# Helical attention on one core: heads taken four apart, feature products first in the scores, clamp and roots moved back

## What is computed

```
q, k, v = x @ Wq.T + bq, x @ Wk.T + bk, x @ Wv.T + bv          # 16 heads of 8 channels
q_hel = einsum('bshd,hed->bshe', qh, Whel) + bhel               # 64 numbers a head and token
k_hel = einsum('bshd,hed->bshe', kh, Whel) + bhel
qn = l2norm(q_hel.reshape(b, s, h, 32, 2)); kn = ...            # 32 unit vectors of 2
# (the two components are then re-paired along the tokens)
helical = einsum('bhpsc,bhptc->bhst', qn, kn) / 32
dot = einsum('bshd,bthd->bhst', qh, kh) / sqrt(8)
attn = softmax(0.5 * dot + 0.5 * helical)
out = (attn @ vh).reshape(b, s, e) @ Wo.T + bo
```

## Time and profile before

| | us |
|---|---|
| runs | 4297.06, 4308.48, 4308.74; median 4308.48 |
| profiled execution | 4305.09 |
| its span, first to last instruction | 4303.4 |
| granted TensorE clock, mean of the span | 0.864 |
| busy: PE, DVE, ACT, POOL | 3207.1, 2627.0, 1840.7, 1635.4 |
| phase `lm`, first instruction | 2586.21 |
| phase `lo`, first ACT operation to last DVE operation | 3335.12 to 3350.90 |

### The profile page before, as it was taken

How to read it: one execution, slowest core, us unless ns; L and a number is a source line. 1 busy time by engine, 2 the same in 40 slices (tenths; PEclk the granted TensorE clock), 3 DMA queues, 4 the chain that set the end, 5 groups by cost and what they waited for, 6 DMA issues and landing times. The chain is left out here.

```text
span 4303.4 us, 87712 instructions
## 1 busy us (share of the span) xinstructions
PE 3207.1 (75%) x22928; PEld 2524.5 (59%) x22928; DVE 2627.0 (61%) x8135; ACT 1840.7 (43%) x5245; POOL 1635.4 (38%) x2885
## 2 busy tenths in 40 slices
PE   6999999999973849999964756777776685333176
PEld 5888888888862737777753624555554473222155
DVE  5666666666651466666651535666664456999954
ACT  4555556555541325555531324555554333111123
POOL 2222222222216624444427604333432250666533
PEclk9999999999985979999975877888888797666578
DMA  8100000000011310000003200000000120000003
GB/s 138 27 0 4 4 4 1 4 4 0 4 31 57 92 27 2 5 2 4 3 31 89 78 5 17 18 16 18 18 18 14 42 61 20 1 1 1 1 18 90
DMA packets 154383, 104.45 MB, mean 24 GB/s; under 512 B 26160, under 2 KB 144192, under 8 KB 153984
## 3 DMA queue, kind: packets, MB, share of 16 engines
q1 hardware_dynamic: 141056, 75.70, 8.2%
q0 software_dynamic: 13184, 27.19, 1.8%
HBM read 45.86 MB, written 43.87 MB: 21 GB/s over the span
## 5 line engine op out<-in xcount | busy, mean ns | idle before, releaser
L351 POOL TENSOR_TENSOR aa_prob<-aa_prob,aa_inv 128x128 f32<-128x128 f32 (+1 forms) x512 | 249.2, 508 | 919.2 <-DVE aa_inv L567 919.2
L661 POOL TENSOR_TENSOR ab_prob<-ab_prob,ab_inv 128x128 f32<-128x128 f32 (+1 forms) x512 | 248.8, 507 | 334.2 <-DVE ab_inv L816 327.6
L374 PE MATMUL aa_proj<-aa_xs,aa_w 128*128 128x256 f32 x1280 | 362.3, 398 | 13.6 <-DMA aa_w<-in_L_attn_a_W_qkv 12.2
L784 ACT ACTIVATE ab_prob<-ab_ps_score,ab_low 128x128 f32<-128x128 f32 (+1 forms) x512 | 211.7, 424 | 303.6 <-PE ab_ps_turn L718 301.6
L482 ACT ACTIVATE aa_qkv<-aa_proj 128x512 f32<-128x512 f32 x384 | 229.4, 597 | 259.1 <-PE aa_proj L374 198.4
L1778 POOL TENSOR_TENSOR lm_sq<-lm_comp 128x512 f32<-128x512 f32 x128 | 161.2, 1259 | 398.7 <-DVE lm_comp L1945 392.4
L2238 PE MATMUL dr_bank<-da_rT,da_spread 128*128 (+1 forms) x256 | 96.3, 464 | 249.9 <-ACT dr_RW L2256 242.3
L2288 POOL TENSOR_TENSOR dr_toward<-dr_S,XN 128x64 f32<-128x64 f32 x512 | 180.6, 371 | 223.7 <-DVE dr_S L2317 160.8
L1934 DVE TENSOR_REDUCE lm_low<-lm_ps_score 128x2 f32<-128x512 f32 x256 | 164.2, 683 | 152.8 <-PE lm_ps_score L1830 152.8
L374 PEld LDWEIGHTS aa_proj<-aa_xs,aa_w 128*128 128x128 f32 x1280 | 213.8, 191 | 46.0 <-issue 13.8
L540 DVE SCALAR_TENSOR_TENSOR aa_look<-aa_th_look,aa_ahead 128x384 f32<-128x384 f32 x256 | 183.4, 716 | 89.2 <-ACT aa_th_look L488 89.2
(11 more groups left out here) (510 smaller groups left out, 9719.8 us busy)
## 6 DMA issues: line engine op xcount, KB each, us to landing
rt_pairs<-rt_empty SPq DMA_DIRECT2D x2, 4615.0 KB, 44.3
rt_slots<-rt_empty SPq DMA_DIRECT2D x2, 2515.5 KB, 45.0
fa_xin<-rt_back SPq DMA_DIRECT2D x8, 512.0 KB, 7.2
fb_xin<-rt_back SPq DMA_DIRECT2D x8, 512.0 KB, 7.2
lm_staged<-la_stack SPq DMA_DIRECT2D x32, 128.0 KB, 2.2
lm_feat<-la_qk SPq DMA_DIRECT2D x256, 16.0 KB
XN<-lm_outT SPq DMA_DIRECT2D x256, 8.0 KB
XNT<-lm_outT SPq DMA_DIRECT2D x256, 8.0 KB
```

The lines of the kernel that those rows point to most:

```text
L351: ins = nc.gpsimd.tensor_tensor(prob[:, h, a:b], prob[:, h, a:b], inv[:, h, t:t + 1].broadcast_to([P, b - a]), ALU.mult)
L374: ins = nc.tensor.matmul(proj[:, i * SEQ:(i + 1) * SEQ], w[:, m, :], xs[:, k, :], start=True, stop=True)
L661: ins = nc.gpsimd.tensor_tensor(prob[:, h, a:b], prob[:, h, a:b], inv[:, h, t:t + 1].broadcast_to([P, b - a]), ALU.mult)
L784: nc.scalar.activation(prob[:, h, a:b], ps_score[:, h, a:b], ACT.Exp, bias=low[:, h, t:t + 1], accum_out=total[:, h, t:t + 1]).then_inc(ex ...
```

## The change

A turn now takes heads k, k+4, k+8 and k+12 of a batch instead of four neighbours, and the loop is unrolled by four (`KINDS`) instead of two. That lets the whole k side of `feat` be one DMA of 128 rows, and the results stay in `stack` and `qk` (whose columns are used up by then) until SP moves them in groups of four batches; the last group's 48 moves fall in phase `lo`, half on ACT's queue ahead of its first logarithm. `feat` has four buffers, `staged` two, and `wh` is gone. The weights of the layer are loaded at the end of `latent_attention` (class `HelicalWeights`: `load` on SP, `clear` on POOL), so that phase `ls` waits for no DMA.

The diff, cut to what is spoken of:

```diff
@@ latent_attention
                     sp.dma_start(wo[:], w_out[bass.ds(p * P, P), :]).then_inc(wo_in, 16)
+                hw.load(sp, hel_zeroed, hel_loaded)
...
                 nc.gpsimd.tensor_scalar(wqs[:], wqs[:], SCALE, None, ALU.mult).then_inc(wq_scaled, 1)
+                hw.clear(nc, pool, hel_zeroed, hel_picked)
                 pool.wait_ge(lat_ok, CHUNKS)
@@ helical_attention, phase ls
                 def _(pe):
-                    pe.wait_ge(loaded, 128)
...
-                    pe.wait_ge(hloaded, 16 * 4 * HEADS)
                     turn(1)
@@ phase lm, sync
+                    def features(m, b, k):
+                        reached(sp, score_mm, UNITS * (m - 3))
                         for u in range(UNITS):
+                            head = UNITS * u + k
+                            sp.dma_start(feat[32 * u + HD * k:32 * u + HD * k + HD, k, 0, :],
+                                         qk[head * HD:(head + 1) * HD, 0, bass.ds(b * SEQ, SEQ)]).then_inc(feat_ok[k], 16)
+                        sp.dma_start(feat[:, k, 1, :], qk[:, 1, bass.ds(b * SEQ, SEQ)]).then_inc(feat_ok[k], 16)
...
+                    def turn(g, i):
+                        b, k = g * GROUP + i // KINDS, i % KINDS
+                        m = 4 * b + k
+                        if k % 2 == 0:
+                            stage(m, b, k // 2)
+                        features(m, b, k)
+                        if i >= 8 and (not isinstance(g, int) or g > 0):
+                            sp.wait_ge(out_ok, 16 * g)
+                            for n in range(4 * (i - 8), 4 * (i - 8) + 4):
+                                move_out(sp, g - 1, n, moved)
@@ phase lm, tensor
+                    def score(m, k):
+                        j = k % 2
+                        pe.wait_ge(feat_ok[k], 16 * (UNITS + 1) * (m // KINDS + 1))
+                        reached(pe, exp_ok, 8 * m)
+                        for c in range(2):
+                            for u in range(UNITS):
+                                rows = slice(32 * u, 32 * u + 32)
+                                nc.tensor.matmul(ps_score[:, u, c * SEQ:(c + 1) * SEQ], feat[rows, k, 0, c * P:(c + 1) * P],
+                                                 feat[rows, k, 1, :], start=c == 0, stop=False)
                         for i in range(2):
                             pe.wait_ge(unit_ok, 2 * m + i + 1)
-                            reached(pe, exp_ok, 8 * (m - 1) + 4 * i + 4)
...
-                        if live(w, TURNS):
-                            attend(w, 1 - j)
                         if live(a, TURNS):
-                            score(a, 1 - j)
+                            score(a, (k - 3) % KINDS)
+                        if live(w, TURNS):
+                            attend(w, (k - 5) % KINDS)
@@ phase lm, vector
-                        if live(r, TURNS):
-                            clamp(r, 1 - j)
                         if live(a, TURNS):
                             maximum(a, 0)
                             maximum(a, 1)
+                        if live(r, TURNS):
+                            clamp(r, (k - 1) % 2)
@@ phase lo, scalar
                 def _(act):
+                    for i in range(MOVES // 2):
+                        move_out(act, GROUPS - 1, i, moved_too)
                     for c in range(CH):
+                        if c == CH - 2:
+                            act.wait_ge(moved, LANDED // 2)
```

More of the change, by code:

```diff
@@ L1553, in helical_attention @@
+def helical_attention(nc, sh, hw):
     HD, HX = 8, 64
@@ L1580, in helical_attention @@
             CH = TOK // 512
             with nc.Block() as block:
[L1582 to L1610, removed]
@@ L1726, in outputs @@
-                    def outputs(half, b, r):
-                        o = 2 * BATCH * half + 2 * b + r
-                        sp.wait_ge(out_ok, o + 1)
-                        for u in range(UNITS):
-                            head = 8 * half + 4 * r + u
-                            for buf, row in ((heads, 32 * u), (totals, 32 * u + HD)):
-                                sp.dma_start(buf[head * HD:(head + 1) * HD, bass.ds(b * SEQ, SEQ)],
-                                             outT[row:row + HD, r, :]).then_inc(moved[r], 16)
@@ L1736, in stage @@
-                    def stage(n):
-                        reached(sp, hel_mm, 2 * n)
-                        sp.dma_start(staged[:], stack[:, :, bass.ds(n, 1), :].rearrange("p a z s -> p a (z s)")
-                                     ).then_inc(staged_ok, 16)
-                    def step(half, b, last=False):
-                        for r in range(2):
-                            if not isinstance(b, int) or b >= 2:
-                                outputs(half, b - 2, r)
-                            elif half > 0:
-                                outputs(half - 1, b + BATCH - 2, r)
-                            features(half, b, r)
-                            if r == 0 and not last:
-                                stage(half * BATCH + b + 1)
@@ L1752, in _ @@
-                    sp.wait_ge(bare, 1)
-                    stage(0)
-                    for half in range(2):
-                        step(half, 0)
-                        step(half, 1)
-                        with sp.Fori(2, BATCH - 1) as b:
-                            step(half, b)
-                        step(half, BATCH - 1, half == 1)
-                    for b in range(BATCH - 2, BATCH):
-                        for r in range(2):
-                            outputs(1, b, r)
-                    for r in range(2):
-                        sp.wait_ge(moved[r], 16 * 2 * UNITS * (TURNS // 2))
+                            head = UNITS * u + k
@@ L1766, in _, with values @@
+                    sp.wait_ge(bare, 1)
+                    for i in range(16):
+                        turn(0, i)
+                    with sp.Fori(1, GROUPS) as g:
+                        for i in range(16):
+                            turn(g, i)
+                    sp.wait_ge(moved, LANDED * (GROUPS - 1))
                 @block.gpsimd
                 def _(pool):
-                    def values(o, j):
+                    def values(o, k):
                         nc.gpsimd.tensor_copy(
-                            vq[:, j, :, :, 0:HD],
-                            v[:, bass.ds((o // 2) % BATCH * 2, 2), bass.ds((o // (2 * BATCH)) * 64 + 32 * j, 32)]
-                            .rearrange("p t (u d) -> p t u d", d=HD)).then_inc(vq_ok, 1)
+                            vq[:, k % 2, :, :, 0:HD],
+                            v[:, bass.ds(o // 4 * 2, 2), :].rearrange("p t (u k d) -> p t u k d", u=UNITS, k=KINDS)[:, :, :, k, :]
+                        ).then_inc(vq_ok, 1)
@@ L1920, in body @@
                         if live(a, TURNS):
-                            for u in range(UNITS):
-                                exps(a, u)
+                            exps(a, 0)
+                            exps(a, 1)
+                        if live(r, TURNS):
+                            inverse_root(r, (k - 1) % 2)
+                        if live(a, TURNS):
+                            exps(a, 2)
+                            exps(a, 3)
                         if live(o, TURNS):
```

237 lines of the change are left out of this document (140 added, 97 removed).

## The result

The changed kernel takes 4283.29 us (median of 5 runs, 4276.37 to 4287.65), the kernel before in the same comparison 4306.83 (4292.49 to 4308.74): ratio 0.9954, 95% interval 0.9933 to 0.9974. The forecast was 4290, between 4237 and 4348. Timed a second time, beside other kernels, the ratio was 0.9969 (0.9958 to 0.9980). So the change makes the kernel 0.3 to 0.5% faster, as forecast; the terms of the sum came out less evenly than the sum, and a part of the gain lies where none was forecast.

What follows compares the result with a forecast made beforehand. The prediction took the loop's ring of waits through attend, scores, copies and exponentials, plus a price for the clock, to bound the kernel; -14.1 - 6.2 + 1.0 + 3.7 = -15.6 from 4305.1 gave 4290 us, range 4237 to 4348.

Steps and rivals of the forecast that it cites:

- The ring: Loop: the chain of waits through exponentials, roots, features, units, attend, transposes and copy takes 9.61 us against 9.83; -14.1 us.
- The clock's price "as it is": Loop: 1.35 us a turn, for PE's halved clock after idling and for `staged` waits, stays unchanged.
- The moves, `staged` and `wh`, "credited none": Loop: fewer DMAs on SP and more buffers are hidden and gain nothing; bound -20 us.
- The loads: Phase `ls`: without weight loads PE begins at once instead of waiting for the last of eight; -6.2 us.
- The clearing: Before the loop: POOL clears four `feat` buffers instead of two while the first DMAs wait; +1.0 us.
- The clamp: DVE in the loop: put behind two maxima, it still comes in time for the roots; costed at nothing.
- The end: Phase `lo`: ACT issues 24 DMAs before its first logarithm, at 0.65 us each; 28.5 us against 24.8, +3.7 us.
- A: Loop: the price of the clock shrinks and waits for `staged` vanish, around 4250 us; chance 0.25.
- B: Loop: every turn starts at 1.2 GHz, 11.7 to 12.0 us a turn, 4337 to 4356 us; chance 0.25.
- C: Loop: slower exponentials or a late clamp take most of the 14 us gain, 4298 to 4305 us; chance 0.15.

Runs made afterwards that it cites:

- the old orders: The changed kernel with the instruction orders of PE, ACT and DVE put back as in the kernel before: 4289.07 us, 0.9981.
- The late-staged run: The changed kernel with the load of `staged` held back until the helical products of the turn just before are done: 4277.74 us, 0.9940.
- the two kernels with orders alone: The kernel before with only the change's PE, ACT and DVE orders, 4328.23 us, 1.0051; the same with roots behind all exponentials, 4337.29 us, 1.0071.
- filling PE's gap: The changed kernel with each turn's four helical products made twice, as surplus work for PE: 4210.23 us, 0.9783.
- late roots: The changed kernel with the two roots behind all eight exponentials instead of in their middle: 4136.93 us, 0.9625.

## Why the forecast was right, step by step

**The ring** was right: 9.61 forecast, 9.52 to 9.54 found, 9.80 with the old orders in the same surroundings. The shape was right too: taking the 1.28 us of roots out of it gave 1.06 a turn.

**The clock's price "as it is"** is the step that does not hold. With the old orders it is 44.38/4 - 9.80 = 1.30 us a turn, with the new 44.38/4 - 9.54 = 1.56: in the cycle of four turns the price takes up the whole gain of the ring. What the new orders gave the loop, they gave by the pairs of 9.53 and 11.01 that break the cycle in some executions. Timed, they are worth 0.9981 - 0.9954 or 0.9981 - 0.9969, 12 or 5 us, with intervals that overlap; so the -14.1 was too large, and where the orders gained, they gained on the clock's cycle and not by a shorter turn at a fixed price. The kernel before already hinted at that: the 9.83 us of the earlier trace rows, taken for the turn at the high clock, came once in its 63 steps from attend to attend; all others but the last four took 10.9 to 12.5.

**The moves, `staged` and `wh`, "credited none"**, is the term mis-sized the other way. The loop with the old orders is 10 us shorter than before (730.4 for 740.6), half of the bound of 20 that the earlier trace rows gave for the waits for `staged`. That compares one profile with one, while executions of the kernel before ranged over 20 us, from 4291 to 4312; the timed 8 us, with -6.3 for the loads, +10.2 for the end and -7.1 behind the layer, leave some 5 for the loop. The late-staged run shows that the second buffer did not remove the waits; it speaks for SP's shorter queue, which was not isolated. That the orders need the rest of the change shows in the two kernels with orders alone: they lose 22 and 31 us, the second by a late `staged`, the first by a cycle that stays open. The two errors have opposite signs; so the loop's -13.1 was found as -20.8 in one profile and -8.8 in the other.

**Behind the layer** the forecast had no term, and -7.5 to -7.9 us were found. Together with an end that cost 6 us more than forecast, this makes the total a sum of errors that happened to cancel: 4290 was met to 7 us, in part by luck, while the layer alone gave -20.1 in one profile and -5.4 in the other for the forecast's -15.6.

**The loads**: -6.2 forecast, -6 to -9 found. Their hiding place held: SP had issued the last of them at 2175.4, and POOL's last work of that phase ends at 2201.2. **The clearing**: 1.80 for 0.95, +0.9 for the forecast +1.0. **The clamp**: at nothing, as forecast; no wait for it in the changed kernel.

**The end** was mis-sized: +9.8 for +3.7. ACT needed 19.5 us for its 24 DMAs, 0.81 each, not SP's 0.65, and could do nothing else meanwhile. That a second issuing engine saves issuing time and nothing more (the Trainium skill, DMA: Bandwidth & Descriptors, "Issuing engines are not separate DMA queues") fits: 24 on each side took 19.0 and 19.5 us side by side; that it saves nothing more was not tested here. And from the last pair's end, 3325.62, to the last addition's, 3330.27, it took 4.65 instead of 2.62.

**The rivals.** A (a smaller price of the clock) is what other kernels do, by filling PE's gap (70 us) and, for half of its 140 us, by late roots, but not this change. B (every turn slow) came nearest with PE's old order and the roots in the middle, 12.0 to 13.6 us a turn, though one attend in four still ran at full clock there. The rule put behind it (the Trainium skill, TensorE: Matmul & The Clock Gate, "HAM oscillation — how this bites in real kernels") is of a loop whose bursts of products take less time than the waits between them; here PE works 7.18 us of a fast turn of 9.52 and is idle 2.34, so the prediction should not have taken it for this loop, and no run here has its every burst starting at half clock. C is close to what the cycle of four does to the ring's gain.

## What to carry to other kernels

Where an engine's clock follows its idle stretches, the ring of waits at full clock is not yet the time of a turn: ask how long the engine idles in it, and move work that others must wait for out of that gap first; moving 1.3 us of roots was worth 115 to 140 us here. Check a new order together with the queues that feed it: the same order that is 161 us faster than the kernel before with the rest of the change is 31 us slower without it. Profile a kernel with such a clock twice, since a loop of 64 turns came out at 719.7 and 731.8 us with the same code. And compare the profiles outside the changed layer too, over all runs: 7.5 us that could pass for scatter in one pair of profiles were there in every pair.

## What the runs showed of the hardware

In two kernels the granted clock alternated in a fixed cycle of four turns whose sum, 44.38 us, was the same for two rings that differ by 0.26 us a turn. With PE idle 2.34 us ahead of the features the mean clock was 0.86 in one profile and 0.84 in the other of the same code, with 3.4 us (ahead of attend) 0.80, with 1.28 to 1.49 it was 0.98 to 1.00, and 60 us of surplus products were paid back more than once. DMAs issued by ACT took 0.81 us each in a row and SP's beside them 0.79; SP's moves in the kernel before took 0.65 to 0.71. DVE stood still for 1.5 to 1.8 us at one instruction of an unchanged layer in three kernels and not in eleven others, for a reason that the traces do not show.
